# A two-layer cross-attention kernel: nine parts of each batch's first layer in steps of four score blocks

## The chip, the cores and the metric

The kernel runs as one program on one core of a Trainium2 chip. The metric is the device time of that program in microseconds, the median of several runs. The engines are TensorE (PE, matrix products; its weight loads are listed as PEld), VectorE (DVE), ScalarE (ACT), GpSimdE (POOL) and SyncE (SP), which here only issues DMAs. Each engine executes its own list of instructions in order and waits on semaphores that the others raise.

## The reference: two cross-attention layers

Input x is 4 x 1024 x 512 and the context 4 x 1024 x 384, all in f32; four batches are independent. Cut to what matters here:

```python
# layer 0: 16 heads of 64; inner width 1024
h = layernorm(x, gamma, beta)
Q, K, V = h @ Wq, ctx @ Wk, ctx @ Wv
attn = softmax(Q K^T) * 64**-0.5          # over 1024 keys, no scale inside
x = x + (attn V) @ Wo + bo
# layer 1: 16 heads of 32; inner width 512
q, k = rotate(rmsnorm(x) @ wq), rotate(ctx @ wk)   # then each scaled to unit length
x = x + (softmax(q k^T * sqrt(32)) v) @ wout
```

In layer 0 the scores are not bounded, so the softmax needs the maximum of each query's scores before the exponential. That makes two sets of score products: a first, rough one, only for the maxima, and a second, precise one, whose exponentials are used.

## The kernel before

**Turns, parts, blocks.** A turn is the work of 128 columns of the inner width, that is two heads in layer 0 (8 turns a batch) and four in layer 1 (4 turns a batch). Each turn has two parts, (turn, half of the queries); `HALVES` lists all parts in order. In a part there are eight blocks of 128 keys (`kt` = 0 to 7). A block of layer 0 is: precise scores on TensorE (`scored`, L698: four products for each of two heads, 64 rows of the array each, so that the two heads' products run side by side; 128 keys by 512 queries by 2 heads), one exponential over both heads on ScalarE (L810) into a ring of eight buffers `probs`, an addition to the running sum of the denominators on VectorE (`added`, L885), and the product with V on TensorE (`attend`, L710: one f32 product a head, 64 columns of the array each, the heads side by side; the trace lists each f32 product as two), which accumulates in `o_acc`.

**Banks.** `scores` is four PSUM banks, two blocks. `scored` for block u waits until the exponential of block u - 2 is done. `work` is three PSUM banks for everything else. The maxima's products (`rowmax`, L666, entries "R") always take banks 0 and 1 together: two products of 64 rows, 512 keys each, for 128 queries and two heads. VectorE then reduces both banks to `tile_max` (L864) and so frees them.

**Steps.** `make_plan` writes the order of work as a list of steps; every engine walks the same list (`run`). In layer 0 a part has four steps of two blocks. A step, as TensorE executes it:

1. `scored` for the blocks of the *next* step,
2. `first` (one R in most steps), `early`,
3. `attend` for this step's own blocks,
4. `fill`: the other products in `work`: projections q, k, v of a later turn (L731, L737), the transposed maxima T (L758), the denominators den (L769), the output projection out (L780),
5. `rest`: mostly one R.

VectorE walks the list too (`on_vector`): the reductions of `first`, then `early` (the reciprocals `recip`, L983, and the multiplication by them `norm_o`, L894), then the additions L885 of *all* blocks of the step, then what `fill` asks of it (the residual additions L972 after out, the low halves L962 after q and k), then the reductions of `rest`. Where the last entry of `fill` is q or k, `rest` stands ahead of it. In steady state a part's four steps have in their `fill`:

- half 0: (out, T, den), (out, q), (out, v), (out, v)
- half 1: (out, T, den), (out, q), (out, k), (out, k)

`recip` is in `early` of the second step, `norm_o` in `early` of the third, which the first out of the third step needs. Eight Rs belong to a part, two a step, for the turn after. In the first parts of a batch, (0, 0) and (0, 1), some of the outs are absent; (0, 1) has (T, den), (q), (out, k), (out, k).

**Denominators.** den goes to `sums` on ScalarE, by DMA to DRAM and back across the partitions (L586, L590), is inverted on VectorE (`recip`), goes to DRAM (L596) and comes back by four DMAs (L601) as `recip`, which norm_o waits for. SP issues them in the order of the list.

**Which bank.** `number` gives each entry of `fill` its bank:

```python
                free = range(BANKS)
                if st.rest:
                    free = (2,) if at_end else (0, 1)
                free = [b for b in free if last[b] is None or last[b].full is not None]
                e.banks = (min(free, key=lambda b: (last[b].full if last[b] else 0, b)),)
```

So in a step with `rest` only the last entry of `fill` gets bank 2; the others take bank 0 or 1, whichever was filled longer ago. Before a product writes a bank, TensorE waits (`claim`) until the last user's reader, on ScalarE or VectorE, is done. For out that is the residual addition L972, for q and k the subtraction L962, for R the reduction L864, for T, v and den a copy on ScalarE.

Of the kernel before, what the change touches and what calls it, by code (L numbers as in the profile page):

```python
# [34 lines left out]
TURN = [(b, l, p) for b in range(B) for l in (0, 1) for p in range((TURNS0, TURNS1)[l])]  # L35
# [10 lines left out]
HALVES = [(b * (TURNS0 + TURNS1) + t, n) for b in range(B) for t, n in ORDER]  # L46
# [7 lines left out]
class Entry:  # L54


    def __init__(self, kind, t, i=0):
        self.kind, self.t, self.i = kind, t, i
        self.full = self.act = self.dve = self.high = self.rope = None
        self.banks, self.before = (), ()  # L60
        self.cols, self.led = P, False


WORK = ("R", "T", "q", "k", "v", "kr", "qr", "kT", "qT", "den", "den_end", "out", "ct", "xt")
# [4 lines left out]
def E(kind, t, *which):  # L69
    return [Entry(kind, t, i) for i in (which or (0,))]  # L70
# [7 lines left out]
def rowmaxes(t, half):  # L78

    return [Entry("R", t, (half, n, qt)) for n in range(2) for qt in range(HT)]  # L80


def transposed(l, b, half, *cs):
    return [Entry("xt", (b, l), (c, half)) for c in cs]


def context(b, *ts):
    s = []
    for t in ts:
        s += E("ct", b, t)  # L90
        if b > 0 and t + C_RING < TT:
            s += E("load_c", b, t + C_RING)
    return s


class Step:


    def __init__(self, t=None, n=None, kts=(), late=False):
        self.t, self.n, self.kts, self.late = t, n, kts, late  # L100
        self.first, self.early, self.fill, self.rest = [], [], [], []


def layer0_beside(b, p, n, t):

    nx, ah = t + 1, t + 2
    if p < 6:
        if n == 0:
            return [E("T", t, 1) + (E("k", nx, 1) if p == 0 and b > 0 else []), E("q", nx, 1), E("v", nx, 0), E("v", nx, 1)]
        return [E("T", nx, 0), E("q", ah, 0), E("k", ah, 0), E("k", ah, 1)]  # L110
    t6, t7, t8, t9 = (b * (TURNS0 + TURNS1) + i for i in (6, 7, 8, 9))
    return {(6, 0): [E("T", t6, 1), E("q", t7, 1), E("v", t7, 0) + E("T", t7, 0), E("v", t7, 1)],
            (7, 0): [[], E("kr", t8, 0), E("kr", t8, 1), []],
            (6, 1): [E("T", t7, 1), [], E("kT", t8, 0, 1), E("norm_a", (b, 1), 0)],
            (7, 1): [E("kr", t9, 0) + transposed(1, b, 0, 0, 1, 2, 3) + lead("v", t8, 0) + E("qr", t8, 0),
                     E("v", t8, 0) + E("v", t8, 1), E("qT", t8, 0) + E("kr", t9, 1), []]}[p, n]
# [38 lines left out]
def maxima_beside(t, n):  # L155

    b, l, p = TURN[t]
    if l == 1:
        if p < TURNS1 - 1 or b == B - 1:
            return [[]] * 8  # L160
        r = rowmaxes(t + 1, 0) + rowmaxes(t + 1, 1)
        ends = (0, 0, 0, 0, 0, 1, 2, 4, 5, 6, 8, 9, 11, 12, 14, 16, 16)
        return [r[ends[8 * n + i]:ends[8 * n + i + 1]] for i in range(8)]
    if p > 5 and n == 1:
        return [[]] * 4
    if (p, n) == (5, 1):
        r = rowmaxes(t + 1, 1) + rowmaxes(t + 2, 0)[:1]
        ends = (0, 2, 5, 7, 9)
    elif (p, n) == (6, 0):
        r = rowmaxes(t + 1, 0)[1:]  # L170
        ends = (0, 2, 5, 7, 7)
    else:
        r = rowmaxes(t, 1) if p == 7 else rowmaxes(t + 1, n)
        ends = (0, 2, 4, 6, 8)
    return [r[ends[i]:ends[i + 1]] for i in range(4)]
# [36 lines left out]
        beside[3][:0] = outs[1:2]  # L212


def make_plan():
    first = Step()
    r = rowmaxes(0, 0) + rowmaxes(0, 1)
    for i, e in enumerate(r):
        e.banks = (BANKS + i % 2 * 2, BANKS + i % 2 * 2 + 1)
    first.fill = (context(0, 0, 1, 2, 3) + E("norm_a", (0, 0), 0) + E("norm_b", (0, 0), 0) + E("k", 0, 0)  # L220
                  + transposed(0, 0, 0, 0, 1, 2, 3) + E("q", 0, 0) + E("norm_a", (0, 0), 1) + context(0, 4, 5, 6, 7)
                  + E("k", 0, 1) + E("norm_b", (0, 0), 1))
    between = [[], [], [], transposed(0, 0, 1, 0, 1), transposed(0, 0, 1, 2, 3), E("q", 0, 1), E("v", 0, 0), E("v", 0, 1),
               E("T", 0, 0), E("k", 1, 0), E("add_bias", 0, 0), E("k", 1, 1), E("q", 1, 0), [], [], E("add_bias", 0, 1)]
    for n, entries in enumerate(between):
        first.fill += r[n:n + 1] + entries
    first.late = True
    steps = [first]
    for j, (t, n) in enumerate(HALVES):
        b, l, p = TURN[t]  # L230
        n_steps = 8 if l else 4
        beside = layer1_beside(b, p, n) if l else layer0_beside(b, p, n, t)
        maxima = maxima_beside(t, n)
        per = KT // n_steps
        half = [Step(t, n, tuple(range(i * per, i * per + per))) for i in range(n_steps)]
        if j > 0 and l == 1:
            (beside[0] if (p, n) == (0, 0) else steps[-1].fill).extend(E("den", *HALVES[j - 1]))
        if (l, p, n) == (0, 7, 1):
            half[0].early += E("norm_b", (b, 1), 0)
        if j > 0:  # L240
            add_results(half, *HALVES[j - 1], beside)
        if j > 1 and TURN[HALVES[j - 1][0]][1] == 0:
            t0, n0 = HALVES[j - 2]
            if TURN[t0][1] == 0 and (TURN[t0][2], n0) != (7, 0):
                for i in range(2):
                    beside[i] = E("out", t0, n0 * HT + 2 + i) + beside[i]
        if (l, p, n) in ((0, 5, 1), (0, 6, 0)):
            beside[2] += beside[1][:1]
            beside[1] = maxima[1][1:2] + beside[1][1:]
            maxima[1] = maxima[1][::2]  # L250
        if (l, p, n) == (0, 6, 0):
            beside[2] = maxima[2][1:] + beside[2][1:] + beside[2][:1]
            maxima[2] = maxima[2][:1]
        for i, st in enumerate(half):
            at = 1 if len(maxima[i]) == 1 and not (l == 1 or (p, n) == (7, 1)) else len(maxima[i]) - 1
            st.first, st.rest = maxima[i][:at], maxima[i][at:]
            st.fill = beside[i]
        steps += half
    end = Step()
    t = N_TURNS - 1  # L260
    end.fill = E("den_end", t, 1) + E("norm_o", t, 1) + E("out", t, 4, 5, 6, 7)
    steps.append(end)

    for kinds, load in ((("q", "qr"), "load_q"), (("k", "kr"), "load_k"), (("v",), "load_v"), (("out",), "load_o")):
        for t in range(N_TURNS - 2):
            st = [st for st in steps if any(e.kind in kinds and e.t == t for e in st.fill)][-1]
            at = [n for n, e in enumerate(st.fill) if e.kind in kinds and e.t == t][-1]
            st.fill.insert(at + 1, Entry(load, t + 2))
    return steps


PLAN = make_plan()


def in_order(st):

    return st.first + st.early + st.fill + st.rest


def on_vector(st):  # L280

    at = max([n for n, e in enumerate(st.fill) if e.kind in WORK], default=0)
    if st.rest and st.fill and st.fill[at].kind in HIGHS:
        return st.first + st.early, st.fill[:at] + st.rest + st.fill[at:]
    return st.first + st.early, st.fill + st.rest


def number():
# [95 lines left out]
def build(nc, rows, x, ctx_in, wq0, wk0, wv0, wo0, bo, gamma, beta, norm_w, wq1, wkv1, wout1,  # L384
# [19 lines left out]
    with ExitStack() as ctx:  # L404
        def sb(name, shape, dt=F32, scope=ctx):
            return scope.enter_context(nc.sbuf_tensor(name, shape, dt))
# [32 lines left out]
        recip = sb("recip", [P, HALF])  # L439
# [89 lines left out]

            return work[:, 0:2, :] if e.banks[0] < BANKS else scores[:, e.banks[0] - BANKS:e.banks[1] - BANKS + 1, :]  # L530

        def run(rowmax, scored, blocks, entry, order=lambda st: (st.first + st.early, st.fill + st.rest)):

            for at, st in enumerate(PLAN):
                after = PLAN[at + 1] if at + 1 < len(PLAN) else None
                if after is not None and not st.late:
                    for kt in after.kts:
                        scored(after.t, after.n, kt)
                ahead, beside = order(st)
                for e in ahead:  # L540
                    (rowmax if e.kind == "R" else entry)(e)
                for kt in st.kts:
                    blocks(st.t, st.n, kt)
                for e in beside:
                    (rowmax if e.kind == "R" else entry)(e)
                if after is not None and st.late:
                    for kt in after.kts:
                        scored(after.t, after.n, kt)
# [97 lines left out]
        def _(pe):  # L646
# [145 lines left out]

            pe.wait_ge(ident_in, 16)
            pe.wait_ge(consts_ok, 1)
            run(rowmax, scored, attend, entry)

        @block.scalar
        def _(act):
# [273 lines left out]
```

## Time and profile before

| | |
|---|---|
| median of 3 runs | 3191.94 us (3189.26 to 3197.08) |
| profiled execution, its own time | 3187.79 us |
| its span, first to last instruction | 3186.0 us |
| TensorE busy | 3045.2 us, 96% of the span |
| VectorE busy | 2302.6 us, 72% |
| ScalarE busy | 1394.3 us, 44% |
| GpSimdE busy | 484.3 us, 15% |
| mean granted TensorE clock | 0.994 |

Busy is the time in which an engine has an instruction in flight. Matmuls overlap, and their ends are modelled, so TensorE's starts tell more than its durations: the time between two starts is the pitch. In a timeline row the first number is the start in us from the span's start, the second the duration; "x2" merges instructions, here the two heads' products that run side by side. A row of TensorE that follows another kind of weights can be listed up to 0.2 us early.

### The profile page before, as it was taken

To read this page: it belongs to the slowest core of one execution; us is meant where nothing else is said; L and a number is where in the kernel's file an instruction comes from. 1 tells how busy PE (TensorE), PEld (TensorE's weight loads), DVE (VectorE), ACT (ScalarE), POOL (GpSimd) and SP (SyncE) were. 2 spreads that over 40 slices of the span, in tenths; PEclk is the share of its full clock that TensorE was granted. 3 is DMA by queue.
4 is the path that set the end of the run, shared out by engine and by line. 5 is a ranking of instruction groups with operands and counts; after the bars stand their busy time and mean duration, and the time that the engine had idled before them with its cause. 6 is when DMAs were issued, how large, how long until landed. Compare 5 with 4: busy or idle time off the path is not lost.

```text
span 3186.0 us, 70506 instructions
## 1 busy us (share of the span) xinstructions
PE 3045.2 (96%) x30408; PEld 1487.2 (47%) x30408; DVE 2302.6 (72%) x2677; ACT 1394.3 (44%) x1473; POOL 484.3 (15%) x221
## 2 busy tenths in 40 slices
PE   7999999999999999899999999999999999999997
PEld 4444445554344444455444444455534444445552
DVE  4777776787777777678677777768766777776766
ACT  2333333556433333356633333345563333334564
POOL 1000002361000000345000000125401000013530
PEclk9999999999999999999999999999999999999999
DMA  3010100111111101021111010101112010010001
GB/s 114 20 26 25 26 22 17 58 31 36 49 48 26 25 25 26 16 58 25 42 60 38 22 26 23 28 17 59 28 38 76 22 26 22 23 25 20 22 19 35
DMA packets 178394, 107.10 MB, mean 34 GB/s; under 512 B 81452, under 2 KB 147116, under 8 KB 178088
## 3 DMA queue, kind: packets, MB, share of 16 engines
q1 hardware_dynamic: 178088, 102.60, 12.1%
q8 instruction: 244, 4.00, 0.5%
q14 instruction: 62, 0.51, 0.1%
HBM read 93.12 MB, written 9.42 MB: 32 GB/s over the span
## 4 chain that ended last, share of the span: by engine, by line
PE 82%; DVE 9%; ACT 3%; issue 3%; DMA 2%; SPq 0%; POOL 0%; DVEq 0%; ACTq 0%
PE o_acc L710 19%; PE scores L698 19%; PE work L737 12%; PE work L731 12%; PE work L780 10%; PE work L666 5%; DVE acc L885 4%; PE work L769 3%; ACT probs L810 2%; DVE tile_max L864 1%; PE work L773 1%; PE work L763 1%; DVE stats L905 1%; PE work L790 1%; DVE sumsq L948 1%
## 5 line engine op out<-in xcount | busy, mean ns | idle before, releaser
L810 ACT ACTIVATE probs<-scores 128x1024 f32<-128x1024 f32 (+1 forms) x768 | 979.6, 1309 | 493.0 <-PE scores L698 485.8
L864 DVE TENSOR_REDUCE tile_max<-work 128x2 f32<-128x1024 f32 x496 | 606.6, 1223 | 414.2 <-PE work L666 413.9
L885 DVE TENSOR_TENSOR acc<-acc,probs 128x1024 f32<-128x1024 f32 (+1 forms) x544 | 859.9, 1581 | 32.4 <-ACT probs L810 9.5
L710 PE MATMUL o_acc<-probs,v_tok 128*64 128x512 f32 (+1 forms) x4096 | 770.9, 607 | 0.2 <-ACT probs L810 0.2
L1003 POOL TENSOR_TENSOR inv<-sumsq,power 128x16 f32<-128x16 f32 x64 | 186.2, 2909 | 1955.1 <-DVE sumsq L950 1955.1
L780 PE MATMUL work<-wo,o_sum 128*32 128x512 f32 (+1 forms) x2072 | 398.6, 598 | 38.1 <-issue 20.1
L698 PE MATMUL scores<-q_high,k_high 32*128 32x512 f32 (+1 forms) x2048 | 384.3, 494 | 16.1 <-ACT probs L810 14.1
L972 DVE TENSOR_TENSOR resid<-work,resid 128x512 f32<-128x512 f32 x384 | 261.6, 685 | 76.1 <-PE work L780 74.2
L710 PEld LDWEIGHTS o_acc<-probs,v_tok 128*64 128x64 f32 (+1 forms) x4096 | 164.5, 122 | 322.7 <-issue 311.5
L698 PE MATMUL scores<-q_low,k_high 32*128 32x512 f32 (+1 forms) x2048 | 307.0, 392 | 0.0
L698 PE MATMUL scores<-q_high,k_low 32*128 32x512 f32 (+1 forms) x2048 | 305.2, 390 | 0.0
L666 PE MATMUL work<-k_high,q_high 64*128 64x512 f32 x992 | 265.7, 532 | 36.3 <-DVE tile_max L864 28.8
L737 PEld LDWEIGHTS work<-wv,cT 128*64 128x64 f32 (+2 forms) x6000 | 262.7, 126 | 69.1 <-issue 68.4
L737 PE MATMUL work<-wv,cT 128*64 128x128 f32 (+2 forms) x6000 | 278.7, 275 | 0.0
L780 PEld LDWEIGHTS work<-wo,o_sum 128*32 128x32 f32 (+1 forms) x2072 | 101.6, 123 | 285.1 <-issue 144.5
L731 PE MATMUL work<-hT,wq 128*64 128x512 f32 (+2 forms) x1144 | 232.5, 593 | 1.7 <-ACT hT L851 1.7
L698 PEld LDWEIGHTS scores<-q_high,k_high 32*128 32x128 f32 (+1 forms) x2048 | 150.4, 187 | 127.0 <-issue 78.6
L698 PE MATMUL scores<-shift,ones_b 64*128 64x512 bf16 x1024 | 201.0, 387 | 0.0
L885 DVE TENSOR_TENSOR acc<-probs 128x1024 f32<-128x1024 f32 (+1 forms) x96 | 157.5, 1641 | 58.5 <-ACT probs L810 58.5
L825 ACT ACTIVATE q_high<-work 128x512 fp32r<-128x512 f32 x96 | 57.5, 598 | 324.5 <-PE work L731 292.6
L666 PEld LDWEIGHTS work<-k_high,q_high 64*128 64x128 f32 x992 | 95.8, 189 | 214.1 <-DVE resid L972 75.4
L731 PE MATMUL work<-cT,wk 128*64 128x512 f32 (+2 forms) x852 | 180.2, 597 | 1.4 <-ACT cT L844 1.4
(80 smaller groups left out, 2463.1 us busy)
## 6 DMA issues: line engine op xcount, KB each, us to landing
recip<-rows_dram SPq DMA_DIRECT2D x380, 64.0 KB, 2.1
stage<-in_x_dram SPq DMA_DIRECT2D x8, 1024.0 KB, 7.5
wq<-in_L_xattn_Wq_dram SPq DMA_DIRECT2D x32, 256.0 KB, 2.8
resid<-in_x_dram SPq DMA_DIRECT2D x8, 1024.0 KB, 5.4
wo<-in_L_xattn_Wo_dram SPq DMA_DIRECT2D x32, 256.0 KB, 2.7
out_dram<-resid SPq DMA_DIRECT2D x8, 1024.0 KB, 4.2
wk<-in_L_xattn_Wk_dram SPq DMA_DIRECT2D x32, 192.0 KB, 2.5
wv<-in_L_xattn_Wv_dram SPq DMA_DIRECT2D x32, 192.0 KB, 2.5
```

What stands on the lines that cost most here:

```text
L666: mm = pe.matmul(maxima_banks(e)[:, h, :], high["q", par][r, tile(half * HT + qt)], high["k", par][r, tokens(n)], start=True, stop=True)
L698: mm = pe.matmul(scores[:, first + h, :], k_rows, qq[r, tokens(n)], start=(i == 0), stop=(i == len(products) - 1))
L710: mm = pe.matmul(o_acc[h * d:(h + 1) * d, :], v_tok[par][:, kt, h * d:(h + 1) * d], probs[:, unit_slot(t, n, kt, h // 2), h % 2, :], start ...
L731: mm = pe.matmul(w[r, :], wt[:, c, r], src[:, c, tokens(e.i)], start=(c == 0), stop=(c == n_c - 1))
L737: mm = pe.matmul(w[r, tile(j)], src[:, c, part(HT * e.i + j, r)], wt[:, c, :], start=(c == 0), stop=(c == n_c - 1))
L769: mm = pe.matmul(w[h * d:(h + 1) * d, :], ones[l][:, 0:d], acc[buffer_of(e.t, e.i)][:, h, :], start=True, stop=(l == 0))
L780: mm = pe.matmul(w[r, :], o_sum[buffer_of(e.t, n)][:, part(e.i % HT, r)], wo[par][:, :], start=True, stop=True)
L810: act.activation(block_probs(t, n, kt), scores[:, 2 * (no % 2):2 * (no % 2) + g, :], ACT.Exp, scale=(1.0, float(D1) ** 0.5 / QK_SCALE ** 2 ...
L864: dve.tensor_reduce(tile_max[:, qt, :, n:n + 1], maxima_banks(e), AX.X, ALU.max, negate=True).then_inc(dve_freed, 1)
L885: dve.tensor_tensor(a, block_probs(t, n, 0) if kt == 1 else a, block_probs(t, n, kt), ALU.add).then_inc(add_ok, units)
L972: dve.tensor_tensor(resid[:, e.i, :], w, resid[:, e.i, :], ALU.add).then_inc(dve_freed, 1)
L1003: pool.tensor_tensor(inv[no % 2][:, :], sumsq[no % 2][:, :], power[:, :], ALU.pow).then_inc(turn_step, 1)
```

## The change

Nine parts of each batch, those after (0, 0) and before (5, 0) in layer 0, that is (0,1), (1,0), (1,1), (2,0), (2,1), (3,0), (3,1), (4,0), (4,1), get two steps of four blocks each in place of four steps of two. `two_as_one` merges steps 0 and 1, and 2 and 3:

- the next step's four blocks of `scored` are issued in a row, and a new list `between` puts the step's first R after the second of them and its second R after the third; the third R is `first`, after the fourth block; the fourth is `rest`;
- `attend` and the additions L885 of four blocks stand together;
- `fill` of the two steps is joined: (out, T, den, out, q), then (out, v, out, v) or (out, k, out, k);
- `recip` goes from `early` to the end of the first long step's `fill`; `norm_o` stays in `early` of the second;
- the last long step of a batch, before (5, 0), has only two blocks of `scored` to issue: there one R is `first`, the second stands after the first step's `fill`, the third before the last k, the fourth is `rest`.

All other parts, and layer 1, keep their steps.

```diff
--- before.py
+++ after.py
@@ -99,6 +99,7 @@
     def __init__(self, t=None, n=None, kts=(), late=False):
         self.t, self.n, self.kts, self.late = t, n, kts, late
         self.first, self.early, self.fill, self.rest = [], [], [], []
+        self.between = []
 
 
 def layer0_beside(b, p, n, t):
@@ -210,6 +211,31 @@
     else:
         beside[2][:0] = outs[0:1]
         beside[3][:0] = outs[1:2]
+
+
+def in_long_steps(t, n):
+
+    _, l, p = TURN[t]
+    return l == 0 and (0, 0) < (p, n) < (5, 0)
+
+
+def two_as_one(a, b, last):
+
+
+    st = Step(a.t, a.n, a.kts + b.kts)
+    maxima = a.first + a.rest + b.first + b.rest
+    recip = [e for e in b.early if e.kind == "recip"]
+    st.early = a.early + [e for e in b.early if e.kind != "recip"]
+    st.fill = a.fill + b.fill + recip
+    if last:
+        st.first, st.rest = maxima[:1], maxima[3:]
+        at = len(a.fill)
+        st.fill[at:at] = maxima[1:2]
+        at = [n for n, e in enumerate(st.fill) if e.kind in WORK][-1]
+        st.fill[at:at] = maxima[2:3]
+    else:
+        st.between, st.first, st.rest = maxima[:2], maxima[2:3], maxima[3:]
+    return st
 
 
 def make_plan():
@@ -255,6 +281,9 @@
             at = 1 if len(maxima[i]) == 1 and not (l == 1 or (p, n) == (7, 1)) else len(maxima[i]) - 1
             st.first, st.rest = maxima[i][:at], maxima[i][at:]
             st.fill = beside[i]
+        if in_long_steps(t, n):
+            last = not in_long_steps(*HALVES[j + 1])
+            half = [two_as_one(half[0], half[1], False), two_as_one(half[2], half[3], last)]
         steps += half
     end = Step()
     t = N_TURNS - 1
@@ -274,15 +303,15 @@
 
 def in_order(st):
 
-    return st.first + st.early + st.fill + st.rest
+    return st.between + st.first + st.early + st.fill + st.rest
 
 
 def on_vector(st):
 
     at = max([n for n, e in enumerate(st.fill) if e.kind in WORK], default=0)
     if st.rest and st.fill and st.fill[at].kind in HIGHS:
-        return st.first + st.early, st.fill[:at] + st.rest + st.fill[at:]
-    return st.first + st.early, st.fill + st.rest
+        return st.between + st.first + st.early, st.fill[:at] + st.rest + st.fill[at:]
+    return st.between + st.first + st.early, st.fill + st.rest
 
 
 def number():
@@ -529,13 +558,15 @@
 
             return work[:, 0:2, :] if e.banks[0] < BANKS else scores[:, e.banks[0] - BANKS:e.banks[1] - BANKS + 1, :]
 
-        def run(rowmax, scored, blocks, entry, order=lambda st: (st.first + st.early, st.fill + st.rest)):
+        def run(rowmax, scored, blocks, entry, order=lambda st: (st.first + st.early, st.fill + st.rest), between=lambda e: None):
 
             for at, st in enumerate(PLAN):
                 after = PLAN[at + 1] if at + 1 < len(PLAN) else None
                 if after is not None and not st.late:
-                    for kt in after.kts:
+                    for i, kt in enumerate(after.kts):
                         scored(after.t, after.n, kt)
+                        for e in st.between[i - 1:i] if i else ():
+                            between(e)
                 ahead, beside = order(st)
                 for e in ahead:
                     (rowmax if e.kind == "R" else entry)(e)
@@ -792,7 +823,7 @@
 
             pe.wait_ge(ident_in, 16)
             pe.wait_ge(consts_ok, 1)
-            run(rowmax, scored, attend, entry)
+            run(rowmax, scored, attend, entry, between=rowmax)
 
         @block.scalar
         def _(act):
```

## Rows read from the trace of the kernel before

**Rows 1.** The page's part 1: busy us (share of span) xinstructions of each engine.
```profile
PE 3045.2 (96%) x30408; PEld 1487.2 (47%) x30408; DVE 2302.6 (72%) x2677; ACT 1394.3 (44%) x1473; POOL 484.3 (15%) x221
```

**Rows 2.** Busy by window: nine parts of the first batch; window, length, engines' busy, clock, DMA.
```profile
104.00:382.00 278.00, 277.10 (x1908) 125.70 (x1906) 206.59 (x235) 102.32 (x126) 0.00 (x0) 1.00 0.10 24
```

**Rows 3.** Timeline of TensorE, step 0 of part (4, 0): start, duration, instruction.
```profile
315.33 0.50 PE L666 MATMUL work<-k_high,q_high 64*128 64x512 f32 x2
315.66 0.39 PE L698 MATMUL scores<-q_high,k_high 64*128 64x512 f32 x2
...
316.36 0.39 PE L698 MATMUL scores<-shift,ones_b 64*128 64x512 bf16 x2
...
317.83 1.94 PE L710 MATMUL o_acc<-probs,v_tok 128*64 128x512 f32 x8
319.60 1.03 PE L780 MATMUL work<-wo,o_sum 128*64 128x512 f32 x4
320.46 0.39 PE L758 MATMUL work<-ident_b,neg_max 128*64 128x128 bf16 x8
320.68 1.03 PE L769 MATMUL work<-acc,ones_scaled 128*64 128x512 f32 x4
321.64 0.50 PE L666 MATMUL work<-k_high,q_high 64*128 64x512 f32 x2
```

**Rows 4.** Timeline of three engines, step 2 of the same part.
```profile
330.31 0.50 PE L666 MATMUL work<-k_high,q_high 64*128 64x512 f32 x2
...
331.86 1.94 ACT L810 ACTIVATE probs<-scores 128x1024 f32<-128x1024 f32 x2 [0.83 <-PE scores L698]
331.99 0.68 DVE L962 TENSOR_TENSOR q_low<-work,q_high 128x512 fp32r<-128x512 f32 x1
...
332.27 0.39 PE L698 MATMUL scores<-shift,ones_b 64*128 64x512 bf16 x2
...
332.82 1.94 PE L710 MATMUL o_acc<-probs,v_tok 128*64 128x512 f32 x8
332.94 1.22 DVE L864 TENSOR_REDUCE tile_max<-work 128x2 f32<-128x1024 f32 x1 [0.26 <-PE work L666]
334.08 0.68 DVE L894 TENSOR_TENSOR o_sum<-o_sum,recip 128x512 f32<-128x512 f32 x1
334.68 2.55 DVE L885 TENSOR_TENSOR acc<-acc,probs 128x1024 f32<-128x1024 f32 x2
334.86 1.08 PE L780 MATMUL work<-wo,o_sum 128*64 128x512 f32 x4
335.74 2.82 PE L737 MATMUL work<-wv,cT 128*64 128x128 f32 x48
337.14 0.68 DVE L972 TENSOR_TENSOR resid<-work,resid 128x512 f32<-128x512 f32 x1
338.49 0.50 PE L666 MATMUL work<-k_high,q_high 64*128 64x512 f32 x2
```

**Rows 5.** Timeline at the start-up, where four blocks of scores follow each other.
```profile
72.47 1.02 ACT L810 ACTIVATE probs<-scores 128x1024 f32<-128x1024 f32 x1 [6.47 <-PE scores L698]
...
73.55 0.50 PE L698 MATMUL scores<-q_high,k_high 64*128 64x512 f32 x2
```

**Rows 6.** Timeline of VectorE, the step of group 3, whose predecessor ends with k.
```profile
317.65 0.68 DVE L962 TENSOR_TENSOR k_low<-work,k_high 128x512 fp32r<-128x512 f32 x1
...
318.25 1.21 DVE L864 TENSOR_REDUCE tile_max<-work 128x2 f32<-128x1024 f32 x1
```

**Rows 7.** Timeline of VectorE in part (6, 1): a reciprocal, and the multiplication that uses it.
```profile
516.33 0.20 DVE L983 RECIPROCAL recip_t<-den_t 128x8 f32<-128x8 f32 x1 [4.30 <-DMA den_t<-rows_dram]
...
521.66 0.69 DVE L894 TENSOR_TENSOR o_sum<-o_sum,recip 128x512 f32<-128x512 f32 x1 [2.10 <-DMA recip<-rows_dram]
```

**Rows 8.** Busy by window, as in group 2: the start-up, and the end.
```profile
50.00:75.00 25.00, 21.05 (x98) 11.29 (x96) 13.54 (x18) 5.79 (x9) 0.00 (x0) 0.93 0.06 17
...
3000.00:3186.00 186.00, 159.48 (x2324) 74.62 (x2316) 129.69 (x120) 101.87 (x76) 47.99 (x22) 0.98 0.09 25
```

## The prediction

> **What bounds the kernel.** I read the busy shares first: TensorE 96%, VectorE 72%, ScalarE 44% [rows 1]. Then the window over the nine parts that are changed, in the first batch: TensorE is busy for 277.1 of 278 us, at clock 1.00 [rows 2]. There is nothing to hide a new wait of TensorE behind: each one there is paid in full. The window of the other batches reads the same, so the change touches 4 x 278 = 1112 us of 3186. Third, the timelines of single steps, for the pitch of each kind of product and for the time from one engine to the next.
>
> I use these constants. A pair of score or maxima products takes 0.2325 us (start 315.66 to 316.36 is three pitches, 0.70) [rows 3], so a block of scores 0.93. Four f32 products of out (two listed pairs) take 0.86, a pair 0.43, T 0.22 [rows 3]; attend of two blocks 1.72 (1.77 until the next start); v is 2.75 less the 0.12 of the turn to the next R = 2.63 [rows 4]; k, six pairs, 2.58; q, eight pairs, 3.44. An R right behind the scores starts one pitch after the last score pair: 332.27 + 0.23 = 332.50. From such a start it is 0.44 to VectorE's reduction (332.94), which takes 1.22; the next VectorE instruction starts 1.14 after it; and TensorE starts 0.10 after VectorE has ended (norm_o ends 334.76, out starts 334.86) [rows 4]. So **R to R cannot be under 0.44 + 1.22 + 0.10 = 1.76 us**, because all of them use banks 0 and 1. Additions: two take 2.55, one 1.22, so the second starts 1.33 after the first; the residual addition starts at their end less 0.09 and takes 0.68 [rows 4].
>
> **What it removes.** Step 0 takes 6.31 us from R to R [rows 3]. Its work is 10 score-like pairs 2.33, attend 1.72, out 0.86, T 0.22, den 0.86 = 5.99. The other 0.32 is the turn from products of 64 rows to products of 64 columns and back. Every merge saves one: 18 in a batch. Also, in the third step out now starts at 334.86, where attend would let it start at 332.82 + 1.77 = 334.59: it waits 0.27 for norm_o [rows 4]; with four blocks of attend ahead of it this goes, 8 times a batch. No instruction on any engine goes or comes; the weight loads by DMA follow their products as before, and SP passes them in the same order, but for recip, costed below.
>
> **What it adds.** I put 0 at the start of the R of `rest`. In a long step, TensorE:
> - Blocks 1 and 2 of the scores as before, R1 at 2.19 (332.50 - 330.31) [rows 4]. Block 3 would start at 2.42, but needs block 1's exponential: exponentials start at 1.55 (331.86) and two take 1.94, so the first ends at 2.52; TensorE follows 0.06 later (72.47 + 1.02 = 73.49, and 73.55) [rows 4, 5]. Start 2.58, a wait of 0.16; end 3.51.
> - R2 would start at 3.51 and may not before 2.19 + 1.76 = 3.95: a wait of 0.44. Block 4 from 4.18 to 5.11 (its exponential was done at 3.49).
> - R3 would start at 5.11 and may not before 3.95 + 1.76 = 5.71: a wait of 0.60. In old steps two Rs are 2.09 us or more apart, and this wait is not there.
>
> Sum 1.2 us a long step, against 0.32 saved. Where k stands at the end of the step before and the maxima are complete (first long step of the four half-0 parts), VectorE comes free only at 318.25 - 315.33 = 2.92 in place of 2.63 [rows 3, 6]: 0.29 more.
>
> Then **bank 0**. In old steps the last entry of `fill` has bank 2 and waits for nothing. Now the middle entries share 0 and 1. Count from r, the start of R3 (5.71). VectorE: reduction r + 0.44, additions from r + 1.58. All additions of the step stand ahead of the residual addition that frees out's bank.
> - First long step (out, T, den, out, q): three additions end at r + 1.58 + 2 x 1.33 + 1.22 = r + 5.46, the residual addition at r + 6.05, den on bank 0 may start at r + 6.15. TensorE gets to it at r + 0.32 (attend) + 3.49 (four blocks) + 0.86 + 0.22 = r + 4.89. Wait 1.26.
> - Second long step (out, v, out, v): norm_o first, then four additions from r + 2.18, end r + 7.39, residual addition until r + 7.98, second out from r + 8.08. TensorE gets to it at r + 3.81 + 0.86 + 2.63 = r + 7.30. Wait 0.78 (0.83 with k).
> - But norm_o is also later than r + 1.58. recip now stands behind the first long step's q and its low half, so it starts about 2.28 (331.99 - 330.31 + 0.60) into the next step. From a reciprocal to the norm_o that waited for it were 5.33 us [rows 7]; that gives 7.61, against r + 1.58 = 7.29: 0.3 more, and 1.1 for the second out. Here the bounds are 0.8 (a chain of under 5 us) and 2.3 (one with 1.2 us more in DMAs); I take 1.1, which the row gives.
>
> **The sum by batch.** First long steps: four of half 0, 4 x (-0.32 + 1.2 + 0.29 + 1.26) = 9.7. Four of half 1, 4 x (-0.32 + 1.2 + 1.26) = 8.6. That of (0,1) has no out ahead of den: 0.9. Second long steps: 8 x (-0.32 - 0.27 + 1.2 + 1.1) = 13.7. The step ahead of (0,1), with four blocks and no R between: 0.38 + 0.04 = 0.4. The last long step, before (5,0), has all of attend early and norm_o late: out waits from 6.0 to 7.61 + 0.68 + 0.10 = 8.39; its additions end at 8.21 + 5.21 = 13.4, the residual addition and k's low half at 14.6, so the R in its fill starts at 14.7 in place of 11.97; the next out waits for that reduction until 16.5, the next R for that out's residual addition until 18.2, then k; the following step starts at 21.2. The two old steps take 2 x 7.81 + 0.27 = 15.9: +5.3. Together 38.6 us a batch, 154 us in all. On the profiled execution's 3187.8 us that is 3342; the median of the runs stands 4 us above that execution, so 3342 to 3346: I say 3344.
>
> TensorE is then busy for some 277 of 317 us in these parts, 87%. A stretch with 159.48 of 186 us busy (86%) had a granted clock of 0.98 [rows 8], which on 1108 us of products would be 22 us more, one with 84% and 0.93 would be 83 us more. My waits are short, mostly under 1.3 us, so I leave it out of the sum and keep it for the range. The Trainium skill ("TensorE: Matmul & The Clock Gate", section "A second HAM failure mode: psum-queue depth-cycling") says that short idles between groups of matmuls, frequent enough, make the clock go back and forth; no row shows it for waits of this kind.
>
> **Rivals.**
> 1. *The merge pays.* The turns are saved (18 x 0.32) and norm_o's wait (8 x 0.27), and VectorE keeps up: 32 us off, 3158. For it: VectorE is idle a quarter of the time [rows 2]. Against it: the idle time isn't where it is needed; the 1.76 us between Rs is a chain through one pair of banks, and R, block, R leaves 1.16 us. It is true only if the waits are under 0.45 us a long step.
> 2. *Only the maxima wait.* If the middle entries of `fill` don't wait (another bank is free, or the residual addition comes sooner than the list has it), 16.6 waits of about 1.2 and the 5.3 go: 154 less 4 x 23 = 62, so 3252.
> 3. *The clock falls too.* The pauses bring the granted clock down, to the 0.98 to 0.93 of [rows 8]: 3366 to 3427.
> 4. *recip comes much later* (queued behind a weight load on SP): 8 norm_o a batch, 1.2 us each, another 38 us: 3382.
>
> **Chances.** Forecast 0.76; the merge pays 0.05; only the maxima wait 0.07; clock 0.07; late recip 0.05. A difference under 0.3% (10 us) can't be told from none; it lies between rivals 1 and 2 and has 0.01. Faster 0.05, slower 0.94. The range: the forecast's own bounds are some 25% of 154 (the unmeasured overlaps of four additions, recip's chain): 3305 to 3375. To take in part of 3 and 4 it goes to 3385; below, to 3295.
>
> **What would show it.** In the changed parts: maxima products about 1.76 us apart, with TensorE waiting for `tile_max` before R2 and R3 (0.4 and 0.6 us); the third block of scores waiting 0.16 us for `probs`; den waiting over 1 us for VectorE's `resid`, and the second out of the next step as well; norm_o waiting for the DMA of `recip`. A part lasts about 35 us in place of 30.9. Wrong would be: parts under 31 us; no waits of L666; den starting right behind T; TensorE's granted clock under 0.97 there; a change in layer 1 or in parts (5,0) to (7,1).

## The result, and the profile after

| | before | after |
|---|---|---|
| median of 6 runs each | 3196.1 us | 3411.65 us (3400.69 to 3415.69) |
| profiled execution | 3187.79 us | 3400.69 us |
| TensorE busy | 96% | 91% |
| mean granted TensorE clock | 0.994 | 0.988 |

The ratio is 1.067, 95% interval 1.066 to 1.069: slower by 212.9 us between the two profiled executions. I had forecast 154 us and a range up to 3385; the way was right, the size was 59 us short. The profiled execution is the fastest of the six; by the medians the miss is 68 us (3411.65 against 3344). One of the four executions of the later kernel all_tail_short (3227.56 us, clock 0.945) was a slow one and is left out of its ratio.

The page's part 1 after, against [rows 1]: the work is the same, instruction for instruction (30408 products, 2677 on VectorE). TensorE's busy time is 60 us longer, some of it a lower clock, some of it the modelled ends of products that stand alone; the rest of the 213 us is idle.

```profile
PE 3104.7 (91%) x30408; PEld 1497.5 (44%) x30408; DVE 2319.1 (68%) x2677; ACT 1400.7 (41%) x1473; POOL 484.6 (14%) x221
```

What TensorE waited for, over the whole execution: total in us, number of waits, longest. Before, in the nine parts of the first batch, this view was empty.

```profile
PE work L697 <- DVE tile_max L895: 61.7, 110, 2.1
PE work L811 <- DVE resid L1003: 47.2, 32, 2.0
PE work L811 <- issue: 36.8, 28, 3.2
PE work L800 <- DVE resid L1003: 34.3, 32, 1.4
PE scores L729 <- ACT probs L841: 15.6, 26, 1.2
PE work L697 <- DVE k_low L993: 11.1, 8, 2.7
```

32 waits of den (L800) and 32 of the second out (L811) for the residual addition are what bank 0 gives: eight each a batch, as counted. They stand for 81 us. The view understates the maxima: R2's later start in the timeline below carries no wait. So the starts have to be read. Here is a second long step after (part (2, 1); the half-0 steps differ in v for k), TensorE and VectorE, against [rows 4]:

```profile
260.80 0.50 PE L697 MATMUL work<-k_high,q_high 64*128 64x512 f32 x2
...
263.08 0.19 DVE L1014 RECIPROCAL recip_t<-den_t 128x8 f32<-128x8 f32 x1
...
263.43 0.50 PE L729 MATMUL scores<-q_high,k_high 64*128 64x512 f32 x2
...
264.71 0.50 PE L697 MATMUL work<-k_high,q_high 64*128 64x512 f32 x2
...
265.04 0.39 PE L729 MATMUL scores<-q_high,k_high 64*128 64x512 f32 x2
...
265.77 2.02 SPq L632 DMA_DIRECT2D recip<-rows_dram  x4
...
266.52 0.50 PE L697 MATMUL work<-k_high,q_high 64*128 64x512 f32 x2 [0.40 <-DVE tile_max L895]
266.95 3.65 PE L741 MATMUL o_acc<-probs,v_tok 128*64 128x512 f32 x16
267.07 1.23 DVE L895 TENSOR_REDUCE tile_max<-work 128x2 f32<-128x1024 f32 x1 [0.60 <-PE work L697]
269.62 0.69 DVE L925 TENSOR_TENSOR o_sum<-o_sum,recip 128x512 f32<-128x512 f32 x1 [1.33 <-DMA recip<-rows_dram]
270.23 5.21 DVE L916 TENSOR_TENSOR acc<-acc,probs 128x1024 f32<-128x1024 f32 x4
```

From the start of the step: block 3 at 2.63 (forecast 2.58), R2 at 3.91 (3.95), R3 at 5.72 (5.71), attend at 6.15 (6.03). R to R is 1.81 us (forecast at least 1.76). norm_o waited 1.33 us for its DMA and started at 8.82 where I had 7.61. From the reciprocal to norm_o it is 6.54 us, not the 5.33 of [rows 7].

A first long step and the bank wait of den, TensorE only:

```profile
253.19 1.03 PE L811 MATMUL work<-wo,o_sum 128*64 128x512 f32 x4
254.05 0.39 PE L789 MATMUL work<-ident_b,neg_max 128*64 128x128 bf16 x8
255.50 1.08 PE L800 MATMUL work<-acc,ones_scaled 128*64 128x512 f32 x4 [1.05 <-DVE resid L1003]
```

Before, den started 0.22 us behind T [rows 3]; here 1.45.

Last, the stretches where the granted clock fell, in the window view of [rows 2]: the end of the last long step of the first batch, and the last k of part (0, 1).

```profile
424.00:430.00 6.00, 6.00 (x18) 1.68 (x18) 1.23 (x1) 0.36 (x1) 0.00 (x0) 0.56 0.00 0
132.00:137.00 5.00, 5.00 (x18) 1.45 (x16) 0.69 (x1) 0.28 (x1) 0.00 (x0) 0.66 0.00 0
```

Of the two levels 1.2 and 2.4 GHz, both windows spent more than half of their time at 1.2 (from 424 to 428 us the view reads 0.50 throughout), right behind waits: in part (0, 1) one of 1.95 us for the residual addition, in the last long step 3.15, 2.67, 1.32 and 0.79 us in a row, the first until norm_o was done (the view lists it as issue), the second for k's low half:

```profile
419.82 0.50 PE L697 MATMUL work<-k_high,q_high 64*128 64x512 f32 x2 [2.67 <-DVE k_low L993]
...
421.64 1.27 PE L811 MATMUL work<-wo,o_sum 128*64 128x512 f32 x4 [1.32 <-DVE tile_max L895]
...
423.70 0.80 PE L697 MATMUL work<-k_high,q_high 64*128 64x512 f32 x2 [0.79 <-DVE resid L1003]
...
424.43 5.16 PE L762 MATMUL work<-cT,wk 128*64 128x512 f32 x12
```

The twelve listed products of k take 5.16 us there, 2.77 at full clock. In the other changed parts of that batch the windows read 1.00, though two of their second outs waited 1.98 and 2.02 us. In the second batch two waits of the same lengths did have a fall behind them; here are the two of 2.02 us, one of each batch, each with the window behind it:

```profile
276.10 1.08 PE L811 MATMUL work<-wo,o_sum 128*64 128x512 f32 x4 [2.02 <-DVE resid L1003]
276.00:281.00 5.00, 4.91 (x28) 1.99 (x30) 2.11 (x4) 0.60 (x1) 0.00 (x0) 1.00 0.01 3
...
1042.45 1.08 PE L811 MATMUL work<-wo,o_sum 128*64 128x512 f32 x4 [2.02 <-DVE resid L1003]
1042.00:1047.00 5.00, 4.55 (x14) 1.44 (x16) 1.68 (x3) 0.00 (x0) 0.00 (x0) 0.66 0.00 0
```

### The profile page after: what moved, and what is told of

It reads as the page before. It is cut to its first block, busy times and chain, and to the rows that moved or that the text cites. A ratio compares the mean times of both kernels' runs of the same rounds, so it can differ in the third digit from the quotient of the medians.

```text
span 3398.9 us, 70442 instructions
## 1 busy us (share of the span) xinstructions
PE 3104.7 (91%) x30408; PEld 1497.5 (44%) x30408; DVE 2319.1 (68%) x2677; ACT 1400.7 (41%) x1473; POOL 484.6 (14%) x221
## 4 chain that ended last, share of the span: by engine, by line
PE 60%; DVE 23%; issue 7%; DMA 6%; ACT 3%; SPq 1%; DVEq 0%; POOL 0%; ACTq 0%
PE scores L729 12%; DVE acc L916 11%; PE o_acc L741 11%; PE work L762 10%; PE work L768 10%; PE work L811 8%; DVE tile_max L895 5%; PE work L697 4%; PE work L800 3%; DMA recip<-rows_dram 3%; DMA rows_dram<-recip_t 2%; ACT probs L841 2%; DVE resid L1003 2%; SPq L632 1%; PE work L804 1%
## 5 line engine op out<-in xcount | busy, mean ns | idle before, releaser
L741 PE MATMUL o_acc<-probs,v_tok 128*64 128x512 f32 (+1 forms) x4096 | 757.5, 607 | 0.2 <-ACT probs L841 0.2
L811 PE MATMUL work<-wo,o_sum 128*32 128x512 f32 (+1 forms) x2072 | 401.9, 603 | 103.7 <-DVE resid L1003 47.2
L811 PEld LDWEIGHTS work<-wo,o_sum 128*32 128x32 f32 (+1 forms) x2072 | 101.6, 123 | 341.2 <-issue 205.3
L762 PE MATMUL work<-cT,wk 128*64 128x512 f32 (+2 forms) x852 | 192.6, 633 | 1.4 <-ACT cT L875 1.4
L856 ACT ACTIVATE k_high<-work 128x512 fp32r<-128x512 f32 x96 | 56.9, 597 | 290.5 <-PE work L762 257.8
```

Source lines behind the costliest of these rows:

```text
L741: mm = pe.matmul(o_acc[h * d:(h + 1) * d, :], v_tok[par][:, kt, h * d:(h + 1) * d], probs[:, unit_slot(t, n, kt, h // 2), h % 2, :], start ...
L762: mm = pe.matmul(w[r, :], wt[:, c, r], src[:, c, tokens(e.i)], start=(c == 0), stop=(c == n_c - 1))
L811: mm = pe.matmul(w[r, :], o_sum[buffer_of(e.t, n)][:, part(e.i % HT, r)], wo[par][:, :], start=True, stop=True)
```

## The experiments

All ratios are to the kernel before, measured beside each; differences between two of them are the difference of their ratios times 3192 us, the kernel before in the first runs.

| kernel | median us | ratio (95% interval) | expected us or ratio |
|---|---|---|---|
| changed kernel | 3411.65 | 1.0673 (1.0661 to 1.0686) | |
| banks | 3321.31 | 1.0401 (1.0384 to 1.0419) | 1.042 |
| recip_early | 3365.71 | 1.0531 (1.0510 to 1.0553) | 1.055 |
| banks_recip | 3294.09 | 1.0317 (1.0301 to 1.0332) | 3275 to 3285, 1.03 |
| tail | 3375.64 | 1.0562 (1.0546 to 1.0578) | 1.058 |
| all_tail | 3273.32 | 1.0260 (1.0242 to 1.0277) | 3270, 1.024 |
| before_short | 3140.92 | 0.9826 (0.9812 to 0.9841) | 0.99 |
| after_short | 3295.52 | 1.0317 (1.0298 to 1.0337) | 1.025 |
| all_short | 3192.52 | 0.9988 (0.9979 to 0.9997) | 10 to 25 us over before_short |
| all_tail_short | 3167.30 | 0.9919 (0.9903 to 0.9936) | 3165 to 3175 |
| norm_first | 3179.75 | 0.9958 (0.9944 to 0.9972) | 0.996 |

**banks.** In `number`, a list of banks given by hand for the long steps; the last long step of a batch keeps the rule.

```diff
+                if st.banks:
+                    free = (st.banks.pop(0),)
...
+        st.banks = {5: [2, 0, 1, 0, 2], 4: [2, 0, 1, 2], 3: [0, 1, 2]}[len(work)]
```

> The changed kernel, but in its long steps the fill's banks are set by hand: (out 2, T 0, den 1, out 0, q 2) and (out 2, v 0, out 1, v 2), so that no entry follows an out on its own bank before the additions are done. Theory (bank 0 waits behind the four additions are real and paid in full): den starts right behind T, the first long step is 1.15 us shorter; the second out starts right behind v, but the last v then waits about 0.75 us for the first out's residual addition, so 1.15 us come off there too. 16 times 1.15 and some 1.7 of clock a batch: about 80 us less than the changed kernel, profiled near 3320, ratio to the kernel before near 1.042. Rival (the maxima's pace sets the step, and what is saved behind it is lost before the next maxima): no change, ratio 1.067.

Measured 87 us under the changed kernel. TensorE, the same two kinds of step:

```profile
244.64 1.03 PE L815 MATMUL work<-wo,o_sum 128*64 128x512 f32 x4
245.50 0.39 PE L793 MATMUL work<-ident_b,neg_max 128*64 128x128 bf16 x8
245.72 1.03 PE L804 MATMUL work<-acc,ones_scaled 128*64 128x512 f32 x4
...
264.63 1.06 PE L815 MATMUL work<-wo,o_sum 128*64 128x512 f32 x4
266.85 2.80 PE L766 MATMUL work<-cT,wk 128*64 128x512 f32 x12 [1.16 <-DVE resid L1007]
```

den starts 0.22 behind T again, the second out without a wait; the last k then waits 1.16 us for the first out's residual addition (I expected 0.75; norm_o's delay is in it too). The bank waits are real and were paid in full: they stood for 81 us, and 87 came off.

**recip_early.** recip stands ahead of the last product of the first long step's fill.

```diff
-    st.fill = a.fill + b.fill + recip
+    st.fill = a.fill + b.fill
+    at = [n for n, e in enumerate(st.fill) if e.kind in WORK][-1]
+    st.fill[at:at] = recip
```

> The changed kernel with recip ahead of the last product of the first long step's fill, not behind it. Theory (late norm_o holds up the additions and so the second out): the reciprocal comes about 2.6 us earlier, no norm_o waits for its DMA any more, 0.9 us come off each second long step and over 2.6 off the last one of a batch: about 40 us less than the changed kernel, ratio to before near 1.055. Rival (VectorE then waits for the sums' DMA and the maxima behind it come late): same or slower than the changed kernel.

Measured 45 us under. VectorE around such a step. In seven of the nine changed parts of the first batch norm_o waits for nothing now; in the first it still waits 0.39 us for its DMA, in the last 1.91:

```profile
256.78 0.20 DVE L1016 RECIPROCAL recip_t<-den_t 128x8 f32<-128x8 f32 x1 [2.36 <-DMA den_t<-rows_dram]
...
263.30 1.22 DVE L897 TENSOR_REDUCE tile_max<-work 128x2 f32<-128x1024 f32 x1 [0.59 <-PE work L699]
264.44 0.68 DVE L927 TENSOR_TENSOR o_sum<-o_sum,recip 128x512 f32<-128x512 f32 x1
```

VectorE did wait for the sums' DMA, as the rival has it, but the maxima behind it are not late: the reciprocal was done before the R of rest.

**banks_recip**, both edits together.

> Both edits on the changed kernel. Theory: only the waits of the maxima (1.04 us a long step), of the third block of scores and the longer turns behind waits remain; about 125 us less than the changed kernel, near 3275 to 3285, ratio to before 1.03. This is what my rival 'only the maxima wait' asked for, which gave 3252. Rival: under 100 us less, if the two waits cover each other.

Measured 114 us under the changed kernel; 87 and 45 would be 132, so the two gains overlap by 18 us, where I had expected next to nothing. The size is not firm: by the four profiled executions (3400.69, 3317.43, 3367.36, 3293.64) the overlap is 9 us.

**tail.** The last long step of a batch without maxima between its products.

```diff
-        st.first, st.rest = maxima[:1], maxima[3:]
-        at = len(a.fill)
-        st.fill[at:at] = maxima[1:2]
-        at = [n for n, e in enumerate(st.fill) if e.kind in WORK][-1]
-        st.fill[at:at] = maxima[2:3]
+        st.between, st.first, st.rest = maxima[:1], maxima[1:3], maxima[3:]
```

> The changed kernel, but the last long step of a batch has no maxima in its fill: its first R stands after the second block of scores, its second and third before attend, the fourth stays in rest. Theory (that step takes 25.3 us because each R of the fill waits for VectorE's additions or residual addition, and the clock falls to half behind these waits): 7 us less a batch, 28 us less in all, ratio near 1.058, and the granted clock stays at 1.00 there. Rival (three Rs in a row wait as long as the two in the fill): no change.

Measured 35 us under the changed kernel. In the first batch the step takes 19.3 us (405.21 to 424.48) in place of 25.3. Over the four batches it is 18.7 in place of 25.4 on average, 27 us in all; the two profiled executions differ by 25 us, the medians by 36. The clock did not stay up, as I had expected it to: it was 0.86 from 412 to 419 us, behind two waits of 1.32 us for tile_max, three Rs in a row.

```profile
409.12 0.50 PE L693 MATMUL work<-k_high,q_high 64*128 64x512 f32 x2 [1.32 <-DVE tile_max L891]
410.94 0.79 PE L693 MATMUL work<-k_high,q_high 64*128 64x512 f32 x2 [1.32 <-DVE tile_max L891]
```

**all_tail**, the three edits together (the last long step gets banks 2, 0, 1, 2 too).

> The changed kernel with the fill's banks set by hand, the early recip, and no maxima in the last long step's fill: the best form of the merge that I have. Theory (the waits are separate and add up): the tail edit gave 36 us on the changed kernel, of which the part due to the late norm_o is already gone here; 20 to 30 us less than banks and recip alone (3294), near 3270, ratio 1.024. What is left above the kernel before is then the pace of the maxima (1.04 us and two longer turns a long step, 68 steps, some 80 us). Rival (the tail's gain came from norm_o): 3290.

Measured 18 us under banks_recip (21 by the medians), at the low edge of what was expected. This is the best form of the merge that I found, and it is still 2.6% behind the kernel before.

**Shorter reductions.** To see what is due to the pace of the maxima, each reduction reads the first 256 of each bank's 512 columns (my first expectation calls it a quarter of the keys; it is half). The maxima over the rest are left out. One reduction then takes 0.69 us, not 1.22.

```diff
-                dve.tensor_reduce(tile_max[:, qt, :, n:n + 1], maxima_banks(e), AX.X, ALU.max, negate=True)
+                dve.tensor_reduce(tile_max[:, qt, :, n:n + 1], maxima_banks(e)[:, :, 0:HALF // 2], AX.X, ALU.max, negate=True)
```

> The kernel before, with each maximum taken over a quarter of the keys (the reduction reads 2 x 256 columns, not 2 x 512 twice over... 1024 in all become 512), so that VectorE is free sooner; the rest of the maxima is left out. It is the control for the next two. Expected: a few waits of TensorE for tile_max and norm_o go, some 20 to 40 us less, ratio near 0.99.

> The changed kernel with the same shorter reduction. Theory (the pace of the maxima, reduction included, and the additions behind the reduction cost the first long step 1.85 us, the second 0.9, since norm_o's DMA holds that one): 110 us less than the changed kernel beyond what the control saves in the other parts; ratio to the kernel before near 1.025. Rival (TensorE waits for something else that falls together with tile_max, the exponentials): under 40 us less.

> The changed kernel with the shorter reduction, the fill's banks set by hand, and the early recip: all three waits are taken away at once. It asks what the merge is worth without them. Rival 'the merge pays' gives 32 us less than the control. My theory: the turn saved (0.32) goes almost whole into the third block's wait for its exponential (0.16 + 0.11 for the turn behind a wait), and the last long step of a batch still loses 5 us: 10 to 25 us more than the control.

> The same with each maximum taken over half of the keys (the rest left out), to compare with the kernel before with that reduction (3141) and with all waits but the tail's taken away (3193). Theory: the merge is worth nothing without its waits, since the third block's wait for its exponential and the turns behind it eat the turn saved: 3165 to 3175, still 25 us over the control. Rival (the merge pays once the waits are gone): at or below 3141.

The control saved 55 us, more than the 20 to 40 expected. The changed kernel with the edit (after_short) saved 114 us: the nine parts are worth some 59 us of that, not 110. The reduction still takes 0.69 us, so R to R cannot be under 0.44 + 0.69 + 0.10 = 1.2 us even so. The first long steps gained 1.4 to 1.6 us (I had 1.85); with recip left late, norm_o's DMA holds up the second ones, which gained less. With the three waits cut down (all_short), the kernel is 51.6 us behind its control, not 10 to 25. The timeline shows where: a first long step takes 15.14 us in place of the 14.99 of two old ones in the control, so no merge pays; and the last long step takes 21.9 us, its last k at half clock. With the tail edit (all_tail_short) the distance to the control is 30 us, near the 25 expected. In all_short, the end of block 2, R1 and the first two products of block 3, then the end of block 4, R3 and attend:

```profile
237.23 0.39 PE L735 MATMUL scores<-shift,ones_b 64*128 64x512 bf16 x2
237.26 0.58 PE L703 MATMUL work<-k_high,q_high 64*128 64x512 f32 x2
237.89 0.50 PE L735 MATMUL scores<-q_high,k_high 64*128 64x512 f32 x2
238.23 0.39 PE L735 MATMUL scores<-q_high,k_low 64*128 64x512 f32 x2
...
239.86 0.39 PE L735 MATMUL scores<-shift,ones_b 64*128 64x512 bf16 x2
240.11 0.50 PE L703 MATMUL work<-k_high,q_high 64*128 64x512 f32 x2
240.54 3.65 PE L747 MATMUL o_acc<-probs,v_tok 128*64 128x512 f32 x16
```

R1 starts one pitch behind 237.23, at 237.46; block 3 would follow at 237.69 and starts at 237.89: a loss of 0.20. Its second product comes 0.34 behind its first, not 0.23: 0.11 more. R3 to attend is 0.43 in place of 0.32: another 0.11. Together 0.42, more than the 0.32 of the turn that the merge saves.

The steps of all_tail_short against those of its control, first batch, say what its 30 us are made of (8.0 us a batch):

| steps | us over the control, a batch |
|---|---|
| the step ahead of (0, 1), without the 1.86 us of the two blocks that it takes over | 0.5 |
| part (0, 1) | 1.3 |
| eight first long steps | 1.2 |
| seven second long steps | 1.4 |
| the last long step, without the two blocks that it gives away | 3.5 |

In the last one two Rs wait 0.79 and 0.78 us for tile_max, and the clock falls:

```profile
362.54 0.51 PE L700 MATMUL work<-k_high,q_high 64*128 64x512 f32 x2 [0.79 <-DVE tile_max L898]
...
363.83 0.49 PE L700 MATMUL work<-k_high,q_high 64*128 64x512 f32 x2 [0.78 <-DVE tile_max L898]
...
365.00:371.00 6.00, 6.00 (x24) 1.90 (x22) 4.56 (x6) 0.60 (x1) 0.00 (x0) 0.77 0.05 17
```

A second long step loses 0.10 to 0.13 us in five of the seven; in the other two, where norm_o waits 0.62 and 0.94 us for its DMA, it loses 0.25 and 0.61. So nearly half of the 30 us is the last long step of a batch, and no kind of long step gains.

**norm_first.** The kernel before, with one edit in VectorE's order for layer 0: norm_o ahead of the first R's reduction.

```diff
+    ahead = st.first + st.early
+    if st.t is not None and TURN[st.t][1] == 0:
+        ahead = [e for e in ahead if e.kind == "norm_o"] + [e for e in ahead if e.kind != "norm_o"]
```

> The kernel before, with norm_o ahead of the first maximum's reduction in VectorE's order, in layer 0 alone; TensorE's order is untouched. Theory (out of the third step waits 0.27 us for norm_o): the wait goes, 13 to 15 times a batch, 12 to 16 us less, ratio 0.996. Rival (the reduction comes 0.6 us later, and out on bank 0 waits for that instead): no change.

Measured 0.9958 (0.9944 to 0.9972), 13 us faster than the kernel before: small, but clear of the interval, and so faster than both. It takes the 0.27 us wait of [rows 4] away without any merge. Out starts 4.28 us into its step (329.10), not 4.55:

```profile
331.38 0.68 DVE L897 TENSOR_TENSOR o_sum<-o_sum,recip 128x512 f32<-128x512 f32 x1
331.98 1.22 DVE L867 TENSOR_REDUCE tile_max<-work 128x2 f32<-128x1024 f32 x1
...
333.38 1.03 PE L783 MATMUL work<-wo,o_sum 128*64 128x512 f32 x4
```

## Why the prediction was wrong in size and right in kind

- **No cover for TensorE's waits.** Right. Each wait that an experiment took away came off the time.
- **The turn saved (0.32).** Not seen by itself: with the short reductions a first long step still takes 0.15 us more than two old ones, and the products read above lose 0.42 us where 0.32 is saved. That longer turns come back behind waits was missed, below.
- **Block 3, R2, R3 (1.2 us a step).** Right: starts within 0.06 us. But a product of 64 rows behind an R that had waited starts 0.33 us later, not one pitch of 0.23 (264.71 to 265.04), and attend 0.43 later, not 0.32 (266.52 to 266.95). That is some 0.1 to 0.2 us a long step against the list of starts; the first long steps came out at 17.5 (half 0) and 17.3 (half 1) against 17.4 and 17.1. Some 5 us in all.
- **den on bank 0 (1.26).** Right; measured start 1.23 later than before, and the edit banks takes it away.
- **recip's chain: the step that failed most.** I took 5.33 us from one row. In the first batch the nine chains were 5.45 to 6.54 us, mean 6.04. The second long steps of the first batch took 17.8 to 18.9 us, mean 18.3, against my 17.7. That is 0.6 us for each, 17 us in all. The mechanism was right, for each of these seven steps is 12.3 to 12.4 us longer than its own chain, as in the forecast (17.7 - 5.33 = 12.4); only the size of the chain was off. I had given 2.3 for the second out's wait as the upper bound; the value was too near to the lower. The change did not make the chain longer. The kernel before has the same chain in the same parts, hidden because nothing waited for it: from the reciprocal to the landing of the last of the four DMAs it took 5.06 to 7.56 us in the 36 parts, mean 5.8, and after the change 5.36 to 6.69, mean 6.0. [rows 7] (5.31 by that measure) was a short one: 28 of the 36 were longer. Much of the spread is the landing of the one write ahead of the four. SP's wait for it, in the nine parts of the first batch, first before, then after (total, number, longest), and the write and the four of [rows 7], where that wait is 518.12 - 516.93 = 1.19 us in place of 1.6 and 1.7 on average:

```profile
SPq L601 <- DMA rows_dram<-recip_t: 14.4, 9, 2.4
...
SPq L632 <- DMA rows_dram<-recip_t: 15.0, 9, 2.5
...
516.56 0.37 SPq L596 DMA_DIRECT2D rows_dram<-recip_t  x1
518.12 1.71 SPq L601 DMA_DIRECT2D recip<-rows_dram  x4
```

- **The last long step of a batch.** Forecast 21.2, measured 25.3 us (24.2, 26.6 and 25.4 in the other batches): norm_o 0.9 later again (it waited 4.68 us), and k at half clock, 2.4. 16 us in all.
- **The step ahead of (0, 1).** Forecast +0.4, measured +2.4 (9.39 us from R to R, 7.00 before). A slip of mine: two blocks of scores, 1.86 us, move from the last long step, where I counted them as gone, into this one, where I did not count them as come. 8 us in all.
- **The clock.** I left it out of the sum for waits of under 1.3 us. It fell in part (0, 1), where k takes 4.44 us in place of 2.77, and in the last long step, where k and out take 2.6 us more: 4.3 us in the first batch, partly counted in the items above. The others are not all like it: taken as length times the missing share of the clock, the changed parts lost 5.1, 6.8, 6.7 and 3.4 us in the four batches, and none in the kernel before. The six runs show it as well: 3400.69 us at clock 0.988, 3415.69 at 0.982. The Trainium skill ("TensorE: Matmul & The Clock Gate", section "A second HAM failure mode: psum-queue depth-cycling") has the clock go back and forth where short idles come often enough. The trace agrees in part: the clock did move, but in most changed parts several waits a step of 0.4 to 1.3 us left it at 1.00, and it fell behind single waits of 1.95 us and more (not behind all of them), or behind a few of 0.8 to 1.3 us close together.

By batch, measured on the first: first long steps 1.3, second long steps 4.1, that of (0,1) 2.8, the last 4.1, the step ahead of (0,1) 2.0 over the forecast, 14.3 in all. From the step ahead of (0, 1) to the end of the last long step the four batches are 53.0, 53.5, 52.0 and 49.3 us longer than before, 207.8 together against the forecast 154: that holds 53 of the 59 us missing. The other 5 lie in parts that the change left alone, where I had forecast none; they weren't taken apart.

By cause, over the four batches, I estimate from these steps: what the chain takes beyond 5.33 us some 24 us (36 chains, 0.66 us each), the clock some 19, the two blocks 8, the turns behind waits 5. So the failed steps are, in this order: the chain taken at 5.33 us where it is 6.0, the clock put at nothing in the sum, and the two blocks not counted where they went.

Of the rivals: *the merge pays* is false, and false even with its waits cut down (all_tail_short is 30 us over its control). *Only the maxima wait* is close to what all_tail builds, and it gives 83 us over the kernel before; I had 62. That sum has a slip too: 16.6 waits of 1.2 us and 5.3 us are 25 us a batch, not 23, which gives 53. *The clock falls too* is true in part, as above. The measured time lies in its range (3366 to 3427), but for the larger part by the chain and the two blocks; that it fits is luck. *recip comes much later* was not it: SP issued the write 0.22 us behind the reciprocal in all 36 parts, and the reciprocal came at the forecast 2.28 us.

What stays open is the clock. Eight second outs of changed parts waited 1.95 to 2.02 us; behind three of them the next 5 us read 0.66, behind five 1.00, and waits of 2.02 us are on both sides. The trace doesn't say what decides it. Open too is how much of the last long step's 3.5 us in all_tail_short is the clock alone.

## What to carry to other kernels

Before joining steps to save turns, write down for every shared buffer the shortest time from one use to the next (here product, reduction, release: 1.8 us) and compare it with the spacing that the new order gives; a quarter of idle time on the other engine says nothing about it. Where work is joined on an in-order engine, whatever stands behind the joined block (here residual additions behind four additions) frees its buffer that much later, so buffers have to be given out anew. A chain through DMAs must be taken as a spread, not as one row, when it becomes what is late next; the trace of the kernel before has all of them, hidden or not, from SP's issues and landings; and when work moves across the edge of a changed stretch, count it once where it leaves and once where it arrives.

## What the runs showed of the hardware

- Behind a product of 64 rows that has waited on a semaphore the next one of the same kind starts 0.33 us later in place of 0.23 (the same 0.33 stands behind the first R of a step, which follows products of 64 columns, [rows 3]), and the turn from 64 rows to 64 columns takes 0.43 in place of 0.32.
- The granted clock stayed at 1.00 through parts in which TensorE waited several times a step. Waits of 1.95 to 2.02 us had a window of 5 us at 0.66 behind them three times and one at 1.00 five times. The clock read 0.86 behind two waits of 1.32 us (tail), 0.77 behind two of 0.79 and 0.78 (all_tail_short), and 0.56 behind 3.15, 2.67, 1.32 and 0.79 us in a row.
- One DMA to DRAM and four back, in a chain from VectorE to VectorE, took 5.45 to 6.54 us within one batch, for the same sizes; the kernel before had the same spread.
- A reduction over 2 x 256 columns took 0.69 us, over 2 x 512 1.22 us: a line through the two leaves 0.16 us that do not go with the columns (an estimate from two points).
